# Weight casts on two queues: the store moves from GpSimd to SyncE, and fewer casts are issued in the first phase

## The reference, cut to what matters

```python
xn = layernorm(x)                                   # x: 16 x 2048 x 1024
q  = xn @ q_w.T + q_b                               # 16 heads of 64
xd = conv1d(xn, conv_w, stride=2) + conv_b          # 1024 keys
k, v = xd @ k_w.T + k_b, xd @ v_w.T + v_b
attn = softmax(q k^T / 8) v @ out_w.T + out_b
e  = argmax(xn @ W_router)                          # 4 experts
h  = gelu(xn @ W1[e] + b1[e])                       # W1: 4 x 1024 x 4096, float32 in HBM
ffn = layernorm(h @ Wo + bo + xn)
out = x + attn + ffn
```

## Time and profile before

| | us |
|---|---|
| median of 2 runs | 4844.51 (4843.74 to 4845.28) |
| the profiled execution, its own time | 4828.88 |
| its span, slowest core (core 0) | 4827.3 |
| spans of the 8 cores | 4795.3 to 4827.3 |
| TensorE busy | 3770.5 (78%) |
| VectorE busy | 2037.2 (42%) |
| ScalarE busy | 1574.6 (33%) |
| GpSimd busy | 183.6 (4%) |

### The profile page before, as it was taken

How to read it: one execution, slowest core, us unless ns; L and a number is a source line. 1 busy time by engine, 2 the same in 40 slices (tenths; PEclk the granted TensorE clock), 3 DMA queues, 4 the chain that set the end, 5 groups by cost and what they waited for, 6 DMA issues and landing times.

```text
span 4827.3 us, 53904 instructions; the slowest of 8 cores (4795.3 to 4827.3 us)
## 1 busy us (share of the span) xinstructions
PE 3770.5 (78%) x15040; PEld 1492.2 (31%) x15040; DVE 2037.2 (42%) x3620; ACT 1574.6 (33%) x2245; POOL 183.6 (4%) x341
## 2 busy tenths in 40 slices
PE   4327999958988878878815789996898888888883
PEld 3203122213333333333314321221333333333331
DVE  3500457713325435345254324674331552552544
ACT  4202456613313223223124223663231331331330
POOL 1110111100000000000000000000000000000000
PEclk9998579969999999999955775998899999999997
DMA  5541444433444444534411110001235244435332
GB/s 124 96 78 35 90 87 86 85 73 140 152 97 157 143 99 151 152 111 157 96 66 36 35 35 0 1 1 53 83 127 144 114 162 109 157 141 121 133 126 69
DMA packets 90180, 473.49 MB, mean 98 GB/s; under 512 B 10976, under 2 KB 11008, under 8 KB 47920
## 3 DMA queue, kind: packets, MB, share of 16 engines
q1 hardware_dynamic: 50464, 318.82, 17.7%
q0 software_dynamic: 39440, 151.22, 17.5%
HBM read 537.15 MB, written 50.33 MB: 122 GB/s over the span
## 4 chain that ended last, share of the span: by engine, by line
PE 53%; DMA 32%; issue 7%; DVE 5%; ACT 2%; SPq 0%; POOL 0%; DVEq 0%; POOLq 0%; ACTq 0%
PE ps L995 29%; DMA castslot<-w 14%; DMA w1r<-scrW 10%; PE ps L1059 6%; DMA wor<-wo 5%; PE psOT L625 3%; PE psS L717 3%; PE psC L515 2%; PE psBC L648 2%; PE psOT L678 1%; DMA rowsl<-rows 1%; PE psC L561 1%; PE psC L537 1%; PE psA_r L391 1%; PE psA_tr L365 1%
## 5 line engine op out<-in xcount | busy, mean ns | idle before, releaser
L995 PE MATMUL ps<-xnT,w1r 128*128 128x512 bf16 x8192 | 1839.2, 384 | 249.3 <-DMA w1r<-scrW 202.8
L995 PEld LDWEIGHTS ps<-xnT,w1r 128*128 128x128 bf16 x8192 | 792.7, 99 | 1292.9 <-issue 398.2
L1004 ACT ACTIVATE gbuf<-ps,b_sb 128x512 bf16<-128x512 f32 x1024 | 701.9, 687 | 1362.7 <-PE ps L995 1119.3
L726 ACT ACTIVATE etb<-psS 128x1024 bf16<-128x1024 f32 x512 | 523.5, 1024 | 393.5 <-PE psS L717 375.5
L1059 PE MATMUL ps<-wor,interT 128*128 128x512 bf16 x2048 | 463.9, 388 | 77.4 <-DMA wor<-wo 69.5
L1013 DVE TENSOR_TENSOR sel<-gbuf,mbc 128x512 bf16<-128x512 bf16 x256 | 108.9, 425 | 831.1 <-ACT gbuf L1004 831.1
L625 PE MATMUL psOT<-etb,v 128*65 128x512 bf16 x1024 | 376.4, 456 | 0.0
L717 PE MATMUL psS<-qT,kT 64*128 64x512 bf16 x1024 | 367.0, 445 | 4.0 <-DVE v L571 2.0
L1059 PEld LDWEIGHTS ps<-wor,interT 128*128 128x128 bf16 x2048 | 200.9, 99 | 340.4 <-issue 117.8
L638 DVE RECIPROCAL arena<-psOT 1x512 f32<-1x512 f32 x64 | 214.5, 3352 | 215.2 <-PE psOT L625 215.0
L365 PE MATMUL psA_tr<-eye_f,arena 128*128 128x128 f32 x256 | 89.9, 444 | 249.0 <-DVE arena L345 114.6
(11 more groups left out here) (103 smaller groups left out, 2692.9 us busy)
## 6 DMA issues: line engine op xcount, KB each, us to landing
w1r<-scrW SPq DMA_DIRECT2D x256, 1024.0 KB, 7.5
wor<-wo POOLq DMA_DIRECT2D x64, 1024.0 KB, 9.0
castslot<-w POOLq DMA_DIRECT2D x128, 256.0 KB, 4.8
scrW<-castslot POOLq DMA_DIRECT2D x128, 256.0 KB, 3.2
arena<-x SPq DMA_DIRECT2D x16, 1024.0 KB, 6.5
arena<-x SPq DMA_DIRECT2D x32, 512.0 KB, 5.9
out<-arena SPq DMA_DIRECT2D x32, 512.0 KB, 2.9
wslot<-qwT POOLq DMA_DIRECT2D x2, 2048.0 KB, 14.1
```

The lines of the kernel that those rows point to most:

```text
L726: E.emit("scalar", lambda s, par_=spar, pair_=pair, eo=eoff: s.activation(etb_t[:, eo + pair_ * 1024:eo + (pair_ + 1) * 1024], ps_s[par_][ ...
L995: t_.matmul(ps8[:, gp_ * 512:(gp_ + 1) * 512], w1r[:, sl_, cc_ * 512 + ic_ * 128:cc_ * 512 + (ic_ + 1) * 128], xnT[:, cc_, 8 + tb_ * 512:8 ...
L1004: E.emit("scalar", lambda s, e_=e, icg_=icg, gp_=gpar: s.activation(gbuf[:, icg_ % 2, e_, :], ps8[:, gp_ * 512:(gp_ + 1) * 512], AF.Gelu, ...
```

## The change

A cast's store is issued by SyncE in place of GpSimd, and has a pair of semaphores of its own (`sCSTO`); the next load into the slot waits for that. In phaseA(0) 3 casts are emitted behind each step in place of 6 (24 in place of 48), and in phaseC(0) 3 behind each head in place of 2 (104 remain, in place of 80). The barrier of phaseB waits for the new semaphores too.

```diff
+    sCSTO = [mksem(f"sCSTO{i}") for i in range(2)]
...
-    cast_state = {"chain": [(sCAST[0], 0), (sCAST[1], 0)], "idx": 0, "ops": []}
+    cast_state = {"chain": [(sCSTO[0], 0), (sCSTO[1], 0)], "idx": 0, "ops": []}
...
             mld = sCAST[sl].n
-            E.emit("gpsimd", lambda g, sl_=sl, d_=dstap: g.dma_start(
+            E.emit("sync", lambda s, sl_=sl, d_=dstap: s.dma_start(
                 d_, cslot[:, sl_, :]),
-                waits=[(sCAST[sl], mld)], incs=[(sCAST[sl], 16)])
-            chain[sl] = (sCAST[sl], sCAST[sl].n)
+                waits=[(sCAST[sl], mld)], incs=[(sCSTO[sl], 16)])
+            chain[sl] = (sCSTO[sl], sCSTO[sl].n)
...
             if b == 0:
-                drain_cast(6)
+                drain_cast(3)
...
-                    dc(2)
+                    dc(3)
...
-        barrier(extra=[(sCAST[0], sCAST[0].n), (sCAST[1], sCAST[1].n)])
+        barrier(extra=[(sCAST[0], sCAST[0].n), (sCAST[1], sCAST[1].n),
+                       (sCSTO[0], sCSTO[0].n), (sCSTO[1], sCSTO[1].n)])
```

## The result

| | before | after |
|---|---|---|
| median of all runs, us | 4857.13 (10 runs) | 4711.69 (11 runs) |
| ratio after to before, with its 95% interval | | 0.9708 (0.9681 to 0.9734) |
| profiled execution, own time | 4828.88 | 4727.1 |
| spans of the 8 cores | 4795.3 to 4827.3 | 4673.3 to 4725.5 |

The median lies 0.4 us from the predicted 4711.3, which is closer than the working deserves: the sum was made against a median of 4844.51, and the two profiled executions are 101.8 us apart, since that of after is the slowest of those counted (4701.01 to 4727.1). Two later comparisons of the same pair, each on another chip, gave ratios of 0.9727 (0.9679 to 0.9774) and 0.9782 (0.9741 to 0.9823).

The account below looks back on a forecast made before the run. Casts holding up q's weights and the first W1 load were taken as the bound. Gains 128.3 + 4.9 = 133.2 us gave 4695.7, for the median 4711.3 us; range 4693 to 4717, for 8 in 10 4693 to 4746.

Parts of the forecast that it names:

- Part 1, the load of q's weights: End of phaseA(0): with 24 casts gone, this load leaves at 194.59 in place of 322.86, gaining 128.3 us.
- Part 1, q to the output weights: After phaseA(0): 167.28 us for b = 0, 165.03 for b = 1; the 2.3 us between were left out as room.
- Part 2: Stores between SyncE's x loads in phaseA(0): hidden in waits of up to 21.0 us, cost nothing; at most 4.8 at the start.
- Part 3: Casts behind the output weights: two slots side by side, 9.0 us a round, ending 21 us ahead of attention; gain 4.9 us.
- The limit of 9.41 us a round: Longest round of two casts in phaseC(0) with which the casts are still hidden behind attention.
- the formula: Casts' end behind attention in phaseC(0): 20.8 + 51 P - 500.8 us, P being the round of two casts.
- Part 4: 3 in place of 2 casts behind each head in phaseC(0): only the place of emission changes; cost and gain nothing.
- What doesn't move: Attention of both batch elements (500.5 and 501.8 us), phaseB(0) and b = 1 as a whole keep their durations.
- Little overlap: Rival on casts in phaseC(0): only the store's issue is saved, 5.58 us a cast, 4800 us; within a shared 10%.
- doesn't do what it says: Rival on casts in phaseC(0): loads still one by one at 6.13 us, 4857 us, 12 us slower; within a shared 10%.
- The slower rival: Rival on casts in phaseC(0): SyncE's stores hold back GpSimd's loads, P 14.5, 4971 us; chance 3%.
- the large term: Gain up to the first W1 load, from q's earlier load and the casts hidden behind attention: 133.2 us.

Follow-up runs that it names:

- the split alone: Kernel before with 3 casts a step in phaseA(0) and 3 a head in phaseC(0), stores still issued by GpSimd; ratio 1.0032.
- the queue alone: Kernel before with stores issued by SyncE, still 6 casts a step in phaseA(0) and 2 a head in phaseC(0); ratio 0.9807.
- the dense matmuls: Against the kernel before: three slots, 3 casts a step, rows' loads on GpSimd, 64 unused full-size matmuls behind the second head of attention's first block; ratio 0.9473.
- three slots on two queues: Changed kernel with three cast slots in place of two and all 128 casts behind the output weights; ratio 0.9764 to the kernel before.
- the one-queue kernel with two slots: Changed kernel with loads and stores both from GpSimd, each load ahead of the previous cast's store; 4851.01 us, kernel before 4829.27.

## Why the prediction was right, point by point

- **Part 1, the load of q's weights.** Right: 194.07, 0.54 us behind the last mask (194.59 was worked out). The second batch element was the right template for it. TensorE's wait for those weights fell from 148.1 us to 21.0.
- **Part 1, q to the output weights.** The prediction kept 2.3 us as room; in fact 4.0 us were lost in this trace, and 1.5 to 3.5 in ten of the eleven later ones in which the load of q leaves at 194 us. (In the eleventh, the changed kernel's second, it is 9.2: cores 2 and 3 run k's matmuls at a granted clock of 0.71, where the others have 0.81 to 0.85.) From the issue to the first matmul, k's weights take 15.4 us on the mean of the cores, before 13.4; v's 14.5, before 13.1. The part that missed is the template: the cores of b = 1 reach this point up to 32 us apart, those of b = 0 before 16 us apart, those of after within 0.9 us at q's load and 3 us at k's. In the kernel with the split alone (2 us apart at q) k's take 14.5 us; with the queue alone (10.6 us apart) 14.1.

  What counts is the neighbour core (0 and 1, 2 and 3, and so on), not all eight. Of the 448 loads of k's and v's weights in all 14 traces, 62 don't overlap with the neighbour's. They land in 12.5 us on the mean and in 13.1 at most, though 38 of them overlap with those of three or more other cores. The 100 that overlap with the neighbour's for over 10 us take 13.2 to 16.2 us, 14.7 on the mean. (Times are counted from the start of each core's span, as if the cores started together.) What the two cores share isn't shown.
- **Part 2, the stores in SyncE's list.** The cost of nothing was right, the reason only in part. The third store of a step was to leave within 9 us of the x load. It leaves 14 to 18 us behind it in the later steps (107.21 + 15.54 - 0.32 = 122.43, x load at 106.74), and 15 to 21 in the first three. A first store that is issued beside the x load lands in 10.1 us (107.21), and the cast load behind it starts that much later. So of 21 us of cover 3 to 6 were left on this core, not 12, and in the first three steps none: the x loads were late, and it cost nothing because ScalarE did not need them yet. The prediction had no term for that second cushion. That sharing does not lengthen the phase was read from 181 and 183 us; those two stretches have granted clocks of 1.00 and 0.50, so they are no clean pair, but the last mask, done at 193.7 us on the mean of the cores where it was at 193.5, bears it out. The upper end of its range, 4711.3 + 4.8, is 4716, not 4717. The run with 6 stores a step shows the cover gone and its price, 42 us on the last mask.
- **Part 3, the rate.** Right in mechanism, a little high in size: a round of 8.64 us against 9.0, and by two errors that partly cancel. From a load's issue to its store's issue it is 5.0 us, not 5.58: the 5.58 of before holds 0.55 us of GpSimd's, and SyncE needs 0.06. From the store's issue to the next load's it is 3.7 us, not 3.4: the store lands in 3.1, and GpSimd's 0.59 comes on top. The casts ended 34 us ahead of attention, not 21. The share came out at 0.63, not 0.68: a cast took 2.7 us of all engines (0.63 x 4.32), not the 3.1 of before; why isn't shown. The limit of 9.41 us a round was tested from both sides: 12.3 us (the split alone) ends 150 us late on the mean, where the formula said 145 for 12.26; 10.4 us (one load in flight) ends 53 us late, and 20.8 + 51 x 10.42 - 501 is 51.
- **Part 4, 3 or 2 behind each head.** Argued, not run. By the kernel's text it is right: 64 heads with 2 casts each still take all 104, and behind the output weights' load the lists of GpSimd and SyncE hold nothing but casts, so both lists come out the same.
- **What doesn't move.** Attention: 499 to 503 us in every run without the dense matmuls, with casts at 3.4 to 6.2 us. Right. phaseB(0) keeps its length: not in this trace, where core 3 takes 1526 us and core 7 1480. TensorE is busy for 1185 us on both, and waits for W1 130.9 and 93.5 us. In the two later traces of the same kernel the mean is 1496 and 1493 us. Before, it was 1485, in the split-alone kernel 1488. But the kernel with three slots on two queues, which reaches this phase as early and with its cores as close together (within 10 us), takes 1489, and the one-queue kernel with two slots 1505. So traces of one and the same phase scatter by 20 us, and the 15.9 us are not shown to belong to the change.
- **The rivals.** "Little overlap" went by 5.58 us a cast, and the run that forces one load at a time gave 5.21: that price was 7% high. The "doesn't do what it says" case is the split alone, forecast at 12 us slower and measured at 1.0032, 15 us, which is not clear of noise. The slower rival had nothing to it: the longest store took 5.1 us, as before.

So the large term was sound, 133.2 us forecast and 125.3 measured at the first W1 load (128.5 from slowest core to slowest core), and what the small ones missed is small. By mean spans the whole kernel gained 108 us, by the three ratios 142, 132 and 105. That the median hit to 0.4 us is luck of how the executions of the two sides fell.

## What to carry to other kernels

When a transfer in the background turns up on the critical path, look first at what stands ahead of the late one in the same list. A list in which each store waits for its load costs each cast the load's whole latency and the store's issue, one load at a time. Another queue for the stores takes it apart, and so does a slot more with an order to suit; check the order against the list, since a load that waits for the last store, put ahead of the next store, wins only 0.3 of 6.2 us. Before moving waiting DMAs into another engine's list, count how long its own DMAs can be held up, and how long what waits for those can: here three stores a step made the first loads late and cost nothing, and six cost 42 us. And set the background work against the cover that hides it as a formula in rounds; when the cover is then made shorter, the same formula says when it fails.

## What the runs showed of the hardware

- A 256 KB store out of the software queue lands in 3.3 us (median, slowest core) when it stands ahead of a load, and in 4.6 when it follows a load of 512 KB by 0.5 us. From the hardware queue it lands in 2.6 us with one load in flight (2.6 to 2.9 over the cores), 3.0 with two (2.8 to 3.1) and 3.7 with three (3.6 to 4.1). The load lands in 5.0 us right behind such a store in its queue, and in 4.4 ahead of it.
- GpSimd issues a store 0.55 us after the load that it waited for has landed, and a load 0.59 us after the store; SyncE issues a store 0.06 us after. These medians are the same on every core in the traces of before and after.
- TensorE stayed at 1.2 GHz through some 170 us of matmuls of 64 rows (scores) and 65 columns (values), in which it was busy for 98% of the time, and rose to 2.4 GHz in a stretch of 16 us of full-size ones; the same attention matmuls behind them ran at 2.4 GHz (two scores in 0.60 us in place of 1.03). In all 8 cores and both batch elements this was so, and moving the dense stretch from the block's end to its second head moved the rise with it.
- A weight load that reads 4 MB lands in 12.5 us when the neighbour core's does not overlap with it (13.1 at most in 62 loads), and in 14.7 us on the mean when it does for over 10 us (100 loads). Overlap with three or more of the other six cores' loads, without the neighbour's, left it at 12.5 us (38 loads).
